# Constant bf16 products on TensorE around the first score products of an attention kernel

## The reference, cut to what matters

```python
x = x + 0.5 * ffn(layernorm(x))       # 8 experts, each token goes to the best one
xn = rmsnorm(layernorm(x))            # 8 sequences, T = 256, D = 128
q, k, v = xn @ Wq.T + bq, xn @ Wk.T + bk, xn @ Wv.T + bv      # 16 heads of 8
scores = q k^T * scale, masked above the diagonal
x = x + xn + softmax(scores) v @ Wo.T + bo
x = x + 0.5 * ffn(layernorm(x))
```

## Time and profile before

| | us |
|---|---|
| median of 3 runs | 368.93 (367.42 to 368.98) |
| the profiled execution | 368.29 |
| its span | 365.4 |
| TensorE busy | 254.2 (70%) |
| VectorE busy | 212.2 (58%) |
| GpSimd busy | 186.8 (51%) |
| ScalarE busy | 136.6 (37%) |

### The profile page before, as it was taken

How to read it: one execution, slowest core, us unless ns; L and a number is a source line. 1 busy time by engine, 2 the same in 40 slices (tenths; PEclk the granted TensorE clock), 3 DMA queues, 4 the chain that set the end, 5 groups by cost and what they waited for, 6 DMA issues and landing times.

```text
span 365.4 us, 7398 instructions
## 1 busy us (share of the span) xinstructions
PE 254.2 (70%) x2338; PEld 192.7 (53%) x2339; DVE 212.2 (58%) x613; ACT 136.6 (37%) x329; POOL 186.8 (51%) x293
## 2 busy tenths in 40 slices
PE   0831876787770983896999999998731677686950
PEld 0730775777760552443555555554720677685950
DVE  3568243444436995874788787856558244354534
ACT  1560221222220580054667676775300222132310
POOL 1304665665642320254787787778104566665640
PEclk9999998888896696558899999999855698989885
DMA  8960111112203077773221120001200211112207
GB/s 227 416 219 7 45 42 39 44 44 36 45 35 116 2 209 233 245 237 132 77 68 50 68 89 5 3 4 30 58 29 2 50 43 47 43 38 36 43 36 230
DMA packets 32529, 31.28 MB, mean 86 GB/s; under 512 B 3121, under 2 KB 28082, under 8 KB 32498
## 3 DMA queue, kind: packets, MB, share of 16 engines
q1 hardware_dynamic: 29494, 24.82, 21.1%
q0 software_dynamic: 2944, 6.04, 6.0%
q10 hardware_dynamic: 60, 0.02, 0.0%
HBM read 18.22 MB, written 12.45 MB: 84 GB/s over the span
## 4 chain that ended last, share of the span: by engine, by line
PE 53%; DVE 19%; DMA 8%; issue 7%; another core or an unknown queue 5%; ACT 3%; POOL 3%; SPq 1%; DVEq 0%; ACTq 0%; POOLq 0%
PE bank L1037 13%; PE bank L1048 12%; PE bank L1123 5%; DVE mh L897 5%; PE bank L1129 4%; PE bank L1187 4%; PE bank L1004 2%; PE bank L1209 2%; PE bank L1029 2%; PE bank L1145 2%; DVE arena L779 2%; DMA ks<-sp_d 2%; DMA arena<-y_d 2%; DMA arena<-xn_d,tok_g 2%
## 5 line engine op out<-in xcount | busy, mean ns | idle before, releaser
L1048 PE MATMUL bank<-experts,arena 128*128 x368 | 56.5, 303 | 17.9 <-ACT arena L546 11.2
L431 POOL DMA_INDIRECT y_d<-ys_sb,tok_s x46 | 47.6, 1036 | 41.2 <-DVE ys_sb L823 33.9
L626 ACT ACTIVATE arena<-bank 128x512 f32<-128x512 f32 x96 | 55.8, 600 | 32.5 <-PE bank L1145 32.4
L1037 PE MATMUL bank<-xsT,arena 128*128 128x128 f32 x368 | 57.5, 307 | 8.0 <-ACT xsT L540 6.2
L1048 PEld LDWEIGHTS bank<-experts,arena 128*128 128x128 f32 x368 | 50.9, 214 | 20.3 <-issue 20.2
L1037 PEld LDWEIGHTS bank<-xsT,arena 128*128 128x128 f32 x368 | 53.0, 222 | 10.1 <-ACT xsT L540 7.1
L425 POOL DMA_INDIRECT arena<-xn_d,tok_g x46 | 44.7, 972 | 20.3 <-issue 12.5
L546 ACT ACTIVATE arena<-bank,arena 128x128 f32<-128x128 f32 x92 | 28.9, 367 | 60.2 <-PE bank L1037 37.1
L805 DVE TENSOR_SCALAR arena<-bank,arena 128x128 f32<-128x128 f32 x92 | 27.9, 345 | 38.6 <-PE bank L1037 21.9
L897 DVE TENSOR_REDUCE mh<-bank 128x2 f32<-128x512 f32 x64 | 42.3, 686 | 10.0 <-PE bank L1129 9.8
L492 POOL TENSOR_SCALAR_AFFINE_SELECT arena<-arena 128x512 f32<-128x512 f32 x64 | 40.2, 635 | 9.7 <-ACT arena L626 9.0
(11 more groups left out here) (116 smaller groups left out, 357.9 us busy)
## 6 DMA issues: line engine op xcount, KB each, us to landing
sp_d<-spl SPq DMA_DIRECT2D x32, 192.0 KB, 3.8
experts<-in_experts SPq DMA_DIRECT2D x8, 578.0 KB, 9.2
qz<-sp_d SPq DMA_DIRECT2D x16, 192.0 KB
ks<-sp_d SPq DMA_DIRECT2D x16, 192.0 KB
xn_d<-xn SPq DMA_DIRECT2D x8, 256.0 KB, 4.2
arena<-y_d SPq DMA_DIRECT2D x8, 256.0 KB, 3.8
x<-in_x SPq DMA_DIRECT2D x4, 256.0 KB, 4.5
out<-x SPq DMA_DIRECT2D x4, 256.0 KB, 2.4
```

The source lines that it names most:

```text
L431: pool.indirect_dma_start(y_d[:, :], bass.IndirectOffsetOnAxis(ap=tok_s[:, t:t + 1], axis=0), ys_sb[:, t % OUT, :], None).then_inc(e_st[f] ...
L626: act.activation(pT[:, g % 2, u, :], bank[2 + u % 2][:, :], ACT.Exp, scale=SCALE).then_inc(a_e, 1)
L1037: mm = pe.matmul(bank[2 + 2 * (k % 2) + c // 2][:, (c % 2) * P:(c % 2 + 1) * P], ew[:, k % WRING, c * P:(c + 1) * P], xsT[:, k % 2, :], st ...
L1048: mm = pe.matmul(bank[6 + k % 2][:, 0:D], hT[:, k % 2, c, :], w2.rearrange("p a c -> p (a c)"), start=(c == 0), stop=(c == HC - 1))
```

## The change

TensorE gets products of bf16 constants whose results nobody reads. Twenty of 512 columns come between the last quad and the first score unit, behind a wait for q_r that makes bank 3 free; one of 512 columns behind each of the 17 units of the lead, into bank 3; one of 256 columns behind each of the 12 units of half steps 0 and 1, into bank 7. No other engine's program and no DMA changes.

```diff
-            def step(g):
+            def step(g, idle=False):
                 b, half = divmod(g, 2)
                 for u in range(NU):
                     n = NU * g + u
                     scores(n + LEAD, n)
+                    if idle:
+                        keep_clock(bank[7][:, 0:256], 1)
...
+            def keep_clock(o, n):
+
+                for _ in range(n):
+                    pe.matmul(o, cb[:, C_ONE:C_ONE + P], cb[:, 0:o.shape[1]], start=True, stop=True)
+
+            pe.wait_ge(q_r, 2 * NQ - 2)
+            keep_clock(bank[3][:, :], 20)
             for n in range(LEAD):
                 scores(n, -1)
+                keep_clock(bank[3][:, :], 1)
...
             for g in range(NG):
-                step(g)
+                step(g, idle=g < 2)
```

## The result

The change made the kernel slower: 379.16 us as a median of 4 executions (379.0 to 380.26) against 368.18 us before (366.65 to 368.98), a ratio of 1.031 with a 95% interval of 1.0265 to 1.0354. I had forecast 369.3 us. The profiled execution took 379.00 us with a span of 377.0 us, 11.6 us more than before's 365.4.

The account below looks back on a forecast made before the run. Bound: SP's DMA list, whose rows for half step 2 land at about 171.8 us. Profiled 368.29 + 0 (all ahead of 172 us) + 0.35 (clock afterwards) = 368.6 us, expected as a median of 369.3; range 367.0 to 371.0.

Parts of the forecast that it names:

- the step on the 20 products: Between quads and lead: 20 products fit the wait for stack 0, cost nothing, leave 1.4 us idle; clock stays 1.0.
- Rival 3: Lead, half steps 0 and 1: clock falls, constants run at 1.2 GHz, 5.8 us behind 172; 374.7 us; chance 0.07.
- Denser work: Lead onward: only 1.4 us idle ahead and constants making TensorE's work denser speak against constants running at 1.2 GHz.
- a fall for a few microseconds would cost less than the slack: Ahead of half step 2: a brief clock fall would cost less than the 2.8 us TensorE can lose there.
- The unit price: Constant product of 512 columns on TensorE: estimated at 0.43 us at 1.2 GHz, 0.22 us at 2.4 GHz.
- SP's list as the bound of half step 2: Start of half step 2: rows queued behind stack 3 land at about 171.8 us, so earlier gains come to 0.
- The slack of 2.8 us: Ahead of half step 2: lead and half steps 0 and 1 may cost up to 2.8 us before anything is lost.
- The lead at full clock: Lead: VectorE's pace, 0.65 us per unit, 11.9 us; waiting for stack 1 leaves 1.3 of 2.6 us gain.
- The fall behind half step 2's restart: After 172 us: clock restarts at 0.5 or falls at once, up to 1.3 us more at 0.5, costing 0.35 us.
- The Trainium skill's price for throttled time: Stretch up to half step 1: time times one minus granted share, 22.4 x 0.5 = 11.2 us saved, about 357 us.

Follow-up runs that it names:

- the last kernel: 27 products ahead of the lead, constants behind units of lead and half steps 0 and 1, half step 2's rows before stack 3, against before: 362.57 us, ratio 0.9807.
- the three last kernels with 27 products: Against before: 27 products without constants behind units, 369.10 us; the same with half step 2's rows before stack 3, 364.78; that with constants behind units, 362.57.

## Why the prediction was wrong

**What failed** is one assumption, in the step on the 20 products: that a hole of 1.4 us leaves the clock at 1.0 through the lead. The hole came out at 1.41 us as worked out; the clock fell 2.7 us behind it, and every constant behind it was paid at 1.2 GHz in the list of the engine that had become the bound. In eight executions of the change one, by its time and mean clock, was spared. The experiments show where the odds come from: with 27 products and the constants kept, the ten executions were all free of the loss; with 27 products and no constants in the lead, the clock fell at 4.2 and 4.4 us. Both belong to it, and even so it fell in one of seven executions of the last kernel.

**Rival 3** is what happened, and I gave it 0.07. Two arguments against it were wrong. "Denser work" behind a hole of 1.4 us is no protection: the clock fell when TensorE had been busy all the 2.7 us of the lead. Nor does it bring the clock back: TensorE was busy for 46 us at 1.2 GHz with gaps of 0.04 us in all, and the clock didn't rise. And "a fall for a few microseconds would cost less than the slack" took for granted that it would rise again soon. Its price was worked out at 5.8 us behind 172 and measured at 10.1 us. The terms were too small: the lead took 21.8 us for 19.9, half step 0 8.3 for 7.8, half step 1 10.2 for 8.3, and I priced nothing for half steps 2 and 3 at half clock, which added 3.0 us. The unit price was off as well: a constant product of 512 columns costs 0.54 and 0.32 us at the two clocks between score units, and I had 0.43 and 0.22 from columns alone. Back to back, the 20 took 4.48 us, as priced (4.4). So between score products each costs about 0.1 us more than its columns; I take that for the changing over from and to them, which no run takes apart.

**SP's list as the bound of half step 2** was right. The start lay 29.5 to 30.2 us behind the first score unit in the kernel before and in three experiments at both clocks (29.9, 29.5, 29.6), and moved to 27.5 when the two loads moved. With 27 products alone it was 31.8 us: there the rows were issued later behind the first score unit (25.8 us, in the others 24.0 to 24.9). From the issue of L366 to the start it is 5.2 to 6.1 us in all five, which ties the start to the queue and not to TensorE. With 27 products and a clock that holds, the change gives the time of before within its interval, as forecast. The slack of 2.8 us was right too, and the constants of the half steps alone used it up.

**The lead at full clock** was wrong, though nothing hung on it. I had it at VectorE's pace with a stand for stack 1 at 150.5 us. TensorE needs 0.32 + 0.44 = 0.76 us for a unit with its constant, more than VectorE's 0.65, and in the two profiles in which the clock held to the lead's end no stand for stack 1 shows. (It does show, with 0.9 to 1.1 us, in the three last kernels with 27 products.) At the end TensorE waits 0.4 to 0.6 us for the first rows of maxima, which I had left out. The lead came out at 14.3 and 14.5 us, not at 11.9 or 13.2.

**The fall behind half step 2's restart** was right: with the clock held up to there it fell 0.4 us after the restart, and with the rows early and no hole it didn't fall.

The Trainium skill's price for throttled time (page "TensorE: Matmul & The Clock Gate", section "Terms") gave 11.2 us for a clock that holds, by my estimate from the busy time. With 27 products it held from 142.8 to 168.8 us, and the ratio was 0.9979: in this stretch the trace disagrees, because the end of the stretch was set by a DMA queue and the constants filled what was won.

**Still open**: what decides, from one execution to the next, whether the clock falls in the lead, and why dense work at 1.2 GHz (score products with constants of either type, constant or real data) brought no rise for 41 to 55 us in five profiles (the last part of it in half step 2 or 3, which have none), while in half step 1 without constants it rose 3.7 to 4.2 us after the start in four profiles and not at all in two others. Other types and real data in the constants didn't change that; a rule isn't shown.

## What to carry to other kernels

Price filler work at the low clock, in full, before counting on the high one: if it doesn't hold the clock, it stands in the bound engine's list at half speed. Then ask what ends the stretch in which the clock would help; here it was two small loads behind a large one in a queue, and moving them gained 1.1% with a program that computes nothing extra. A filler that covers a wait but for its last microsecond is a gamble. Let it reach up to the next real work, look for the waits behind that too, and measure over many executions either way.

## What the runs showed of the hardware

TensorE busy all the time by the profile isn't enough for the high clock: 142.9 to 189.2 us at 1.2 GHz with 0.04 us of gaps. The same list of instructions up to the end of the lead held 2.4 GHz there in one execution and not in another. A profile of one execution shows one of the two outcomes; the times of one kernel on one chip, 370.2 and 382.0 to 385.1 us, show both.
